# Choosing experts inside the token turns, and counting slots before making keys

## The reference

```
logits = x @ gate_weight.T                       # [8192, 32]
probs = softmax(logits)
topw, topi = top_k(probs, 8)
topw = topw / topw.sum(-1, keepdims=True)
oh = one_hot(topi.reshape(-1), 32)
pos = (cumsum(oh, axis=0) * oh).sum(-1) - 1      # place of the token in its expert's buffer
buf = zeros((32, 512, 512)).at[flat_e, pos].set(flat_x, mode='drop')
```

## Time and profile before

| | us |
|---|---|
| median of 3 runs (3407.73 to 3411.59) | 3408.61 |
| the profiled execution, its own time | 3411.21 |
| its span, first to last instruction | 3409.4 |
| PE busy | 3229.7 (95%) |
| PE weight loads busy | 2552.5 (75%) |
| DVE busy | 2731.7 (80%) |
| ACT busy | 1593.3 (47%) |
| POOL busy | 1980.0 (58%) |

### The profile page before, as it was taken

How to read it: one execution, slowest core, us unless ns; L and a number is a source line. 1 busy time by engine, 2 the same in 40 slices (tenths; PEclk the granted TensorE clock), 3 DMA queues, 4 the chain that set the end, 5 groups by cost and what they waited for, 6 DMA issues and landing times. The chain is left out here.

```text
span 3409.4 us, 55189 instructions
## 1 busy us (share of the span) xinstructions
PE 3229.7 (95%) x17324; PEld 2552.5 (75%) x17324; DVE 2731.7 (80%) x5290; ACT 1593.3 (47%) x5449; POOL 1980.0 (58%) x1823
## 2 busy tenths in 40 slices
PE   7999999999979999999999699999999969999997
PEld 5777777777648888888888577777777757678886
DVE  4788888888677878888786489999999867767775
ACT  1776767667521111111111478888888745221111
POOL 1665656656545777777776466666666633333333
PEclk8999999999979999999999899999999989999999
DMA  7345454454465676766766445555455357630111
GB/s 216 99 137 172 122 161 140 135 172 123 139 178 153 173 176 168 166 169 171 178 166 141 110 124 154 149 149 170 133 161 165 101 183 287 232 110 13 25 13 25
DMA packets 284780, 490.95 MB, mean 144 GB/s; under 512 B 54019, under 2 KB 74819, under 8 KB 283779
## 3 DMA queue, kind: packets, MB, share of 16 engines
q1 hardware_dynamic: 243698, 408.87, 39.0%
q0 software_dynamic: 32256, 77.65, 12.3%
q10 hardware_dynamic: 8592, 1.57, 0.3%
HBM read 250.32 MB, written 136.96 MB: 114 GB/s over the span
## 5 line engine op out<-in xcount | busy, mean ns | idle before, releaser
L911 ACT ACTIVATE c_pr<-ps,t_negmax 128x154 f32<-128x154 f32 x1024 | 435.5, 552 | 178.4 <-DVE t_negmax L680 176.4
L911 ACT ACTIVATE t_pr<-ps,t_negmax 128x154 f32<-128x154 f32 x1024 | 435.2, 554 | 104.5 <-DVE t_negmax L680 103.7
L608 POOL TENSOR_TENSOR c_pr<-c_pr,t_inv 128x616 f32<-128x616 f32 x256 | 317.5, 1243 | 236.7 <-DVE t_inv L695 236.3
L608 POOL TENSOR_TENSOR t_pr<-t_pr,t_inv 128x616 f32<-128x616 f32 x256 | 318.7, 1245 | 231.5 <-DVE t_inv L695 230.6
L680 DVE TENSOR_REDUCE t_negmax<-ps 128x4 f32<-128x616 f32 x512 | 403.6, 788 | 45.6 <-PE ps L976 45.2
L703 DVE COPY t_pTm<-ps 128x512 f32<-128x512 f32 x448 | 305.9, 683 | 135.2 <-PE ps L989 135.1
L976 PE MATMUL ps<-t_kst,t_stack 98*128 98x154 f32 x2048 | 352.9, 290 | 18.5 <-DMA t_stack<-t_q_low 9.5
L81 PE MATMUL ps<-e_xT_high,e_wgu_high 128*128 128x512 f32 x768 | 302.8, 394 | 1.4 <-DVE e_xT_low L1504 1.4
L976 PEld LDWEIGHTS ps<-t_kst,t_stack 98*128 98x128 f32 x2048 | 278.9, 193 | 31.6 <-issue 15.6
L83 PE MATMUL ps<-e_xT_high,e_wgu_low 128*128 128x512 f32 x768 | 300.0, 391 | 0.0
L82 PE MATMUL ps<-e_xT_low,e_wgu_high 128*128 128x512 f32 x768 | 299.7, 390 | 0.0
(11 more groups left out here) (373 smaller groups left out, 9264.5 us busy)
## 6 DMA issues: line engine op xcount, KB each, us to landing
t_stack<-t_q_high SPq DMA_DIRECT2D x1016, 64.0 KB, 2.0
c_wgu_in<-in_gate_upT SPq DMA_DIRECT2D x32, 1536.0 KB, 6.4
t_stack<-t_q_low SPq DMA_DIRECT2D x512, 64.0 KB, 2.0
x_dram<-c_wide_rows SPq DMA_DIRECT2D x32, 1024.0 KB, 7.8
c_wd_in<-in_downT SPq DMA_DIRECT2D x32, 768.0 KB, 4.6
t_xbo<-in_x SPq DMA_DIRECT2D x16, 1024.0 KB, 6.9
xw_dram<-t_z SPq DMA_DIRECT2D x16, 1024.0 KB, 5.3
t_xbo<-x_dram SPq DMA_DIRECT2D x16, 1024.0 KB, 10.7
```

The lines of the kernel that those rows point to most:

```text
L608: pool.tensor_tensor(p, p, inv[:, v, :].unsqueeze(1).to_broadcast([P, KEYS, HG]), ALU.mult).then_inc(s["normed"], 1)
L911: op = act.activation(pr[:, u % 4, :, h], flat[:, col:col + KEYS], ACT.Exp, bias=negmax[:, u, h:h + 1], accum_out=total[:, u, h:h + 1])
```

## The change

In the first token stage each turn now makes the choice itself. After the MAX8 operations `logits` subtracts the largest logit (`share`), replaces the eight largest values of each tile by a very low number (`match_replace`, result `others`), compares with the logits (not equal: chosen, `sel`), and writes the difference to the tile before into `step_up`, which now lives across the stages. The two copies are gone. ACT takes the exponential of `share` at step 3 of the next turn; at step 6 DVE multiplies by `sel`, keeps the last tile's `sel`, sums, inverts and multiplies to the weights; SP stores them a turn later, between the stacking of the second and of the third query. After the last turn the weights of the last group are made and stored at the end of the stage, which waits for the stores.

In the slots stage the whole choice on DVE and the store from ACT are gone. PE counts first, as soon as POOL has made the triangle (three results), then makes keys and values; the four banks of the first key jobs are free when the counts in them are evacuated; the two small products stand between key jobs. POOL's table memsets come ahead of the ramps, and DVE waits for ten of POOL's results.

```diff
-def kv_products(pe, ps, k, s, banks, freed, wk_in, ctx_in):
+def kv_products(pe, ps, k, s, banks, freed, wk_in, ctx_in, between=None):
...
     for j in range(KV_JOBS):
         bank = j % banks
-        if j >= banks:
-            pe.wait_ge(*freed(j - banks))
+        if between:
+            between(j)
+        if freed(j):
+            pe.wait_ge(*freed(j))
...
-        LOG = 31
+        LOG, WTS = 31, 6
+        LOWEST = -2.0 ** 127
...
+            def store_weights(j):
+
+                sp.wait_ge(s["weighted"], j + 1)
+                sp.dma_start(rows(scr["xw"], j)[:, :, D:XW], weight[:, j % 2]).then_inc(s["w_stored"], 16)
...
                 if cur:
                     stack_up(i, 1)
+                if 0 <= i - 3:
+                    store_weights(i - 3)
...
             sp.wait_ge(s["x_stored"], 16 * NG)
+            if gate:
+                store_weights(NG - 1)
+                sp.wait_ge(s["w_stored"], 16 * NG)
...
             def logits(j):
...
                 op.then_inc(s["top"], 1)
-                dve.tensor_copy(c["logits"][:, bass.ds(j * TG * E, TG * E)],
-                                logit[:].rearrange("p t e -> p (t e)"))
                 dve.wait_ge(s["top"], j + 1)
-                dve.tensor_copy(c["top8"][:, bass.ds(j * TG * TOPK, TG * TOPK)],
-                                top[:].rearrange("p t k -> p (t k)")).then_inc(s["side_out"], 1)
+                reached(dve, s["chosen"], j)
+                dve.tensor_tensor(share[:], logit[:], top[:, :, 0].unsqueeze(2).to_broadcast([P, TG, E]),
+                                  ALU.subtract).then_inc(s["shifted"], 1)
+                for t in range(TG):
+                    op = dve.match_replace(others[:, t, :], top[:, t, :], logit[:, t, :], LOWEST)
+                op.then_inc(s["others"], 1)
+                dve.wait_ge(s["others"], j + 1)
+                dve.tensor_tensor(sel[:, 1:1 + TG, :], others[:], logit[:], ALU.not_equal).then_inc(s["picked"], 1)
+                dve.wait_ge(s["picked"], 2 * j + 2)
+                dve.tensor_tensor(c["step_up"][:, TG * j:TG * j + TG, :], sel[:, 1:1 + TG, :], sel[:, 0:TG, :],
+                                  ALU.subtract).then_inc(s["stepped"], 1)
+
+            def weights(j):
+                dve.wait_ge(s["shared_out"], j + 1)
+                dve.tensor_tensor(share[:], share[:], sel[:, 1:1 + TG, :], ALU.mult).then_inc(s["chosen"], 1)
+                dve.wait_ge(s["stepped"], j + 1)
+                dve.tensor_copy(sel[:, 0, :], sel[:, TG, :]).then_inc(s["picked"], 1)
+                dve.wait_ge(s["chosen"], j + 1)
+                dve.tensor_reduce(wsum[:], share[:], AX, ALU.add).then_inc(s["summed"], 1)
+                dve.wait_ge(s["summed"], j + 1)
+                dve.reciprocal(wsum[:], wsum[:]).then_inc(s["inverted"], 1)
+                dve.wait_ge(s["inverted"], j + 1)
+                reached(dve, s["w_stored"], 16 * (j - 1))
+                dve.tensor_tensor(weight[:, j % 2], share[:], wsum[:].unsqueeze(2).to_broadcast([P, TG, E]),
+                                  ALU.mult).then_inc(s["weighted"], 1)
...
                     if at == LOG and gate and prev2:
                         logits(j)
+                    if at == WTS and gate and 0 <= j - 1:
+                        weights(j - 1)
...
             unrolled(turn)
+            if gate:
+                weights(NG - 1)
...
+            def share_out(j):
+                act.wait_ge(s["shifted"], j + 1)
+                act.activation(share[:], share[:], ACT.Exp).then_inc(s["shared_out"], 1)
...
+                    if at == WTS - 3 and gate and 0 <= j - 1:
+                        share_out(j - 1)
...
# expert_slots_phase
-        MADE = 13
+        TRI_MADE, TABLE_MADE, MADE = 3, 10, 13
...
             made(pool.tensor_copy(tri[:], ones[:]))
+            assert n_made[0] == TRI_MADE
+            made(pool.memset(table[:, :, P:LOOK], 0.0))
+            made(pool.memset(table[NT:NT + 1, :, 0:P], BIG))
...
+            assert n_made[0] == TABLE_MADE
             made(pool.iota(c["slots"][:], [[1, CAP]], base=0, channel_multiplier=0,
...
-            made(pool.memset(table[:, :, P:LOOK], 0.0))
             made(pool.memset(zero[:], 0.0))
-            made(pool.memset(table[NT:NT + 1, :, 0:P], BIG))
...
         def _(act):
-            act.wait_ge(s["shifted"], 1)
-            act.activation(prob[:], prob[:], ACT.Exp).then_inc(s["exped"], 1)
-            act.activation(edge[:], edge[:], ACT.Exp).then_inc(s["exped"], 1)
+            for q in range(1, 8, 2):
+                act.wait_ge(s["count_mm"], q + 1)
+                act.copy(table[0:NT, 4 * q:4 * q + 4, 0:P], ps[0:NT, (HB + q) % 8, :].rearrange("t (e n) -> t e n", n=P)).then_inc(
+                    s["counted1"], 1)
...
-            act.wait_ge(s["weights"], 1)
-            act.dma_start(scr["xw"][0:NTOK, D:XW].rearrange("(t p) e -> p t e", p=P),
-                          prob[:]).then_inc(s["put"], 16)
-            for q in range(1, 8, 2):
...
-            link(dve.tensor_tensor(edge[:], top8[:, :, TOPK - 1], top8[:, :, 0], ALU.subtract))
...
-            dve.tensor_tensor(prob[:], prob[:], by_tile(ws), ALU.mult).then_inc(s["weights"], 1)
-            value_out(2)
-            dve.wait_ge(s["made"], MADE)
+            dve.wait_ge(s["made"], TABLE_MADE)
             link(dve.memset(table[:, :, P:P + 1], float(P)))
             link(dve.memset(table[0:1, :, P:P + 1], 0.0))
             link(dve.memset(table[NT:NT + 1, :, P + 1:P + 2], 1.0))
-            value_out(3)
-            value_out(4)
             for q in range(0, 8, 2):
...
+            dve.wait_ge(s["wv_in"], 32)
+            for n in range(KV_JOBS - 8):
+                value_out(n)
             dve.wait_ge(s["tabled"], 1)
...
         def _(pe):
-            kv_products(pe, ps, k, s, HB, lambda j: (s["evacuated"], j + 1) if j < 8 else (s["valued"], j - 7),
-                        c["key_weights_in"], c["context_in"])
-            pe.wait_ge(s["made"], MADE)
-            pe.wait_ge(s["stepped"], 2)
+            pe.wait_ge(s["made"], TRI_MADE)
             for e in range(E):
...
+            def bank_free(j):
+
+                if j < HB:
+                    return (s["counted1"], 3 + j // 2) if j % 2 else (s["counted0"], 3 + j // 2)
+                return (s["evacuated"], j - HB + 1) if j < 8 + HB else (s["valued"], j - HB - 7)
+
+            def bases_between(j):
+
+                if j == 2:
+                    pe.wait_ge(s["made"], TABLE_MADE)
+                    pe.wait_ge(s["counted0"], 4)
+                    pe.wait_ge(s["counted1"], 4)
+                    pe.matmul(ps[0:NT + 1, HB, 0:E], ramp_b[:], table[0:NT, :, P - 1], start=True,
+                              stop=True).then_inc(s["based"], 1)
+                if j == 4:
+                    pe.wait_ge(s["parted"], 1)
+                    pe.matmul(ps[0:NT + 1, HB + 1, 0:2 * E], falls[:], parts[:].rearrange("t w e -> t (w e)"), start=True,
+                              stop=True).then_inc(s["falls_mm"], 1)
+
+            kv_products(pe, ps, k, s, HB, bank_free, c["key_weights_in"], c["context_in"], bases_between)
```

More of the change, by code:

```diff
@@ L325, in token_phase @@
             logit, top = sb("logit", [P, TG, E]), sb("top", [P, TG, TOPK])
+            others, share = sb("others", [P, TG, E]), sb("share", [P, TG, E])
+            weight, wsum = sb("weight", [P, 2, TG, E]), sb("wsum", [P, TG])
+            sel = sb("sel", [P, 1 + TG, E], BF16)
         else:
@@ L675, in _ @@
                 dve.memset(tick[:], 0.0).then_inc(s["logit"], 1)
+                dve.memset(sel[:, 0, :], 0.0).then_inc(s["picked"], 1)
             def maximum(i, u):
@@ L953, in _ @@
             unrolled(turn)
+            if gate:
+                share_out(NG - 1)
         @block.tensor
@@ L1146, in expert_slots_phase @@
         bkt = sb("bkt", [P, DC, B])
-        prob, gt, eq, run = (sb(n, [P, NT, E]) for n in ("prob", "gt", "eq", "run"))
-        restart = sb("restart", [P, NT, E])
-        sel, step_up = sb("sel", [P, NT, E], BF16), sb("step_up", [P, NT, E], BF16)
-        edge, z, rz, need, ws = (sb(n, [P, NT]) for n in ("edge", "z", "rz", "need", "ws"))
         ones, tri = sb("ones", [P, P]), sb("tri", [P, P], BF16)
@@ L1159, in expert_slots_phase @@
         s = Sems(nc, ctx, "r", "wv_in tau_in tail scaled kf khigh matmul evacuated lowered valued stored "
-                               "made shifted exped step weights selected stepped count_mm counted0 counted1 based parted "
+                               "made step count_mm counted0 counted1 based parted "
                                "falls_mm tabled put")
         block = ctx.enter_context(nc.Block())
-        MADE = 13
+        TRI_MADE, TABLE_MADE, MADE = 3, 10, 13
         @block.sync
@@ L1270, in value_out @@
                                   ALU.add).then_inc(s["valued"], 1)
-            logits = c["logits"][:].rearrange("p (t e) -> p t e", e=E)
```

(21 more changed lines are left out.)

38 lines of the change are left out of this document (7 added, 31 removed).

## The result

The changed kernel takes 3436.86 us (median of 4 runs, 3433.30 to 3438.68), the kernel before, run beside it on the same chip, 3410.10 (4 runs, 3407.73 to 3414.19). The ratio is 1.0076, with a 95% interval of 1.0058 to 1.0093: slower by 0.8%. The forecast was 3437.2 us, "slower" with a chance of 0.85. The profiled execution has a span of 3436.4 us, 27.0 more than before; the terms forecast for it added up to 28.6.

The account below looks back on a forecast made before the run. Bound: a closed chain without slack, PE unit 15, DVE, ACT unit 0, PE unit 1, in each token turn. Terms 18.9 + 2.7 + 3.9 + 4.2 - 1.1 = 28.6 us gave 3437.2 us against the median, range 3414 to 3456.

Parts of the forecast that it names:

- The closed chain at step 31: Token turn: PE unit 15, DVE, ACT unit 0, PE unit 1 have no slack; DVE work added there lengthens the turn.
- Its size: Step 31: added DVE work of 1.88 us less 0.44 for the removed copies, 1.45 us per turn (1.0 to 2.3).
- POOL's hold: Step 31: the subtraction must wait for POOL, in the middle of two normalizations, another 0.2 us.
- Its place: PE's weight load at unit 1's scores would wait about 1.6 us for ACT instead of 0.22.
- Step 6: Weights of the turn before: five DVE operations, 1.1 us, of which 0.3 reaches each of thirteen turns, +3.9 us.
- The cover of 0.55: Behind step 6, DVE's waits for PE of 0.25 and 0.30 us would absorb 0.55 of the weights' work.
- The last two turns and the end: Turns 15 and 16 pay for step 31, +2.7 us; the last choice, weights and store landing add +4.2.
- Slots stage: Counts first, first key matmul at S+11.2, end at S+53.6 instead of S+54.7: -1.1 us (-4 to +5).
- The sum: Whole kernel: 18.9 + 2.7 + 3.9 + 4.2 - 1.1 = 28.6 us, 3437.2 against the median.
- Hidden turns: Rival, token turns: DVE's 7.7 us idle per turn hides the new work; 3414.4 us, chance 0.11.
- Held up by POOL: Rival, steps 31 and 6: two-input operations wait out POOL operations of 1.2 us; 3461.5 us, chance 0.15.
- Faster, through the slots stage: Rival: PE runs that stage without pause, ending S+45.3, if step 31 costs under 0.1 us; 3402.5 us, chance 0.06.

Follow-up runs that it names:

- the other order: Changed kernel with the slots stage making keys and values first, then the counts, the token stage as it is: 3433.08 us, 1.0065 against the kernel before.
- the later wait: Changed kernel with the wait for the last weights' store moved from the token stage's end into the slots stage's end: 3434.07 us, 1.0067 against the kernel before.
- the doubled work: Changed kernel with the four match-and-replace done a second time at step 31, into a tile nobody reads: 3454.03 us, 1.0125 against the kernel before.

## Why the prediction was right, point by point

**The closed chain at step 31: right, shown.** It was argued from two waits, ACT's 2.21 us and PE's 0.22. Work added there cost the turn one to one (0.66 for 0.66), the same work at step 26 nothing, and what was taken away there, even from the kernel before, came back in full (0.45 for 0.44), until nothing more came (0.03 for 0.5).

**Its size: +1.45 forecast, 1.22 measured.** Of the terms, POOL's hold was 0.2 and is 0.1: its normalization ended at 446.85, and the subtraction took 0.39, alone 0.29 (its shortest in the trace). Four match-and-replace and the wait for the last of them were put at 0.72 + 0.13 and took 0.76, from 446.92 to 447.68; four more of them cost 0.66. That each is two instructions is what the Trainium skill says (page "VectorE: DVE Perf Modes", section "Two Vector instructions with no wait between them"); the trace agrees, with 64 loads of 76 ns and 64 replacements of 171 ns, eight instructions a turn.

**Its place: wrong.** The prediction named PE's weight load at unit 1's scores, waiting about 1.6 us for ACT. That wait stayed at 0.2; PE waits 1.1 us at the transposes ahead of those scores. The four rows were read as one chain through the maximum of unit 0, but the copied tile stands in DVE's order between step 31 and that maximum, and in PE's order the transposes that need its bank stand before the scores. The same work is late for both, and PE meets the tile first. The sum is not touched by this. Whoever had looked for the sign only in PE's waits for ACT would have concluded that nothing had happened; ACT's own wait for the maximum did grow, from at most 2.4 to 3.4 us.

**Step 6: +0.3 forecast, 0.39 measured.** The five operations took 1.31, not 1.1, since the first of them took 0.53 for the 0.29 assumed. The cover of 0.55 was as forecast, and it is there again when the weights are moved; of what exceeds it, about half reached the turn, in the forecast (0.3 of 0.55) as in the measurement (0.39 of 0.76).

**The last two turns and the end: +6.9 forecast, +8.1 measured.** The wait for the tile in the last turns grew from 1.60 to 2.85, as the prediction's step said; the two turns gave 1.7 and 1.9 against the 1.45 and 1.25 of the forecast, which had left step 6 out of them. Some 0.55 of the 1.7 belongs to the clock: with the same work of PE in this turn it took 28.6 us at a granted clock of 0.88 (two of the kernels above) and 29.2 at 0.82 (the kernel after and two others), and the kernel before stood at 0.88. The end is the chain read off and the landing of one store; 1.45 us of it could be hidden.

**Slots stage: -1.1 forecast, -3.9 measured, the largest miss.** The mechanism was right: 40 us of DVE taken away, keys and values now late behind the counts, a pause of 4.58 us (4.5 forecast) for POOL's memset and DVE's casts. Two sizes were off. The first key matmul came at S+9.4, not S+11.2, because the forecast had kept POOL's cast at its old 2.22 us where it takes 0.29. The old one stood beside a large DVE subtraction that the change removes. This is the kernel before, from its timeline:

```profile
955.21 2.37 DVE L1275 TENSOR_TENSOR r_prob<-c_logits,c_top 128x2048 f32<-128x2048 f32 x1
```

It ended at 957.58, the cast at 957.72. And the tail's stores with their landing took 4.3 us instead of the 5.15 of the earlier trace rows. From the first key to the tail's end the forecast said 36.5 and the trace shows 36.5. The pause kept its length because the cast stands ahead of both its ends.

**The sum: 28.6 forecast, 27.0 measured, closer than its terms.** The 13 turns were 0.9 us above the forecast, the last two 0.9 and the end 0.3; the slots stage was 2.8 below, and the stretches that nobody changed another 0.9. Inside the 13 turns the steady distance alone gives 20.3 + 1.3; the other 2.2 are irregular turns, which no term had foreseen. That 3437.2 met 3436.86 so closely is luck; that the loss came from DVE's work at step 31 is not.

**Rivals.** "Hidden turns" is refuted by the turn itself. "Held up by POOL" is right on what happens to such an operation (1.30 us beside a normalization) but not on where: at steps 31 and 6 it cost 0.1 and 0.2. "Faster, through the slots stage" had its saving right in kind: with the pause cut to 1.07 us and the keys at full clock the stage does end near S+45 (45.3 measured with the memset moved, S+45.3 forecast; 43.4 in the other order), but its condition, under 0.1 us at step 31, did not hold.

## What to carry to other kernels

Before adding work to an engine, find the place in its order where it waits and the place where others wait for it, and price the addition by the place: 0.66 us of DVE cost 0.66 or nothing within the same turn, at about 88% of busy time either way. Work whose result is needed late should stand behind the wait, however far from its data; here moving the choice and the weights turned a loss of 0.8% into a gain of 0.1%, and with the slots stage in the other order and the later wait it was 0.3%. Before crediting such a gain to a change, take the same slack out of the kernel before: two copies moved there gave it 0.2%. When long work is removed, also re-price its neighbours: what shared a port or a queue with it gets faster, and the constants that used to be hidden behind it (a memset of 3.5 us) become the first thing that everyone waits for.

## What the runs showed of the hardware

- A two-input operation of DVE and an operation of POOL did not run side by side: 128x128 took 0.29 us alone, 1.30 beside a normalization of 1.30 that had begun 0.15 before it, and ended 0.15 behind it; and the other way round POOL's cast took 2.22 beside DVE's subtraction, ending 0.14 behind it, and 0.29 alone. The Trainium skill has this as an exclusive lock for the whole instruction (page "SBUF — State Buffer", section "SBUF: two separate sides"); the traces agree on both sides. Such time counts as busy: 48.8 us of DVE in the turn of 52.65 us against 47.5 in the one of 54.76, with the same number of instructions.
- Match-and-replace over 32 elements: 76 and 171 ns, overlapping, a pair every 0.16 us.
- The granted clock dips for a moment in some turns. This is such a turn of the kernel after; its waits are those of its neighbours, and it is 1.3 us longer at a clock of 0.97:

```profile
609.57:665.58 56.01, 54.52 (x325) 41.16 (x325) 47.60 (x113) 37.61 (x150) 32.76 (x29) 0.97 0.47 133
```

  The dips go with PE's new wait. The five traces whose turns lack it (the kernel before, the same with its copies moved, and the three with the choice moved) have none in their 60 steady turns. The six with a wait of 1.1 us have four in 72, the one with 1.8 us has five in 12, the five long turns of the doubled work. All nine begin 6.9 to 7.9 us after a gate reduction, 1.2 to 2.3 us behind the end of that wait. So the dips seem to be a further cost of work at step 31, beyond its own length. No run was aimed at this, and why one turn has a dip and its neighbour none stays open.
- Other turns are longer at a clock of 1.00. In the kernel after, the turn from 720.28 takes 55.50 us: PE stood idle for 0.55 us until a score matmul at 752.90, and the last of the third query's stacking DMAs had landed at 752.81. In the turn behind it that DMA landed 1.3 us earlier in the turn, and there was no wait. Over 12 steady turns both kinds together add 1.4 us in the kernel before and 3.6 in the kernel after, so of the +23.7 some 2.2 are neither steady turns (12 x 1.69 = 20.3) nor the 13th (1.3).
